# Sorted tokens of an expert layer in three groups instead of two, gated products moved from VectorE to ScalarE and GpSimd, and a new order of the work beside attention

## The chip, the cores and the metric

One core of a Trainium2 chip runs the whole program. The metric is the device time in microseconds (us) of one execution, as the median of several. The engines are named as the profile names them: PE (TensorE; PEld are its weight loads), DVE (VectorE), ACT (ScalarE), POOL (GpSimd) and SP (SyncE, which issues most DMAs).

## The reference

Input x is [1, 2048, 128], float32. Two layers, each with modulation by a vector c (shift, scale and gate rows from silu(c) @ wmod):

```python
h = layernorm(x) * (1 + ca) + sa
x = x + ga * attention0(h)       # 16 heads of 8, all 2048 keys, softmax
h = layernorm(x) * (1 + cb) + sb
x = x + gb * ffn0(h)
# second layer, its own modulation
x = x + ga * attention1(h)       # 8 query heads of 16, one key/value head, causal
x = x + gb * ffn1(h)             # x mixed with its predecessor, sigmoid(r) * (relu(k)**2 @ W_v)

def ffn0(hidden, ...):
    logits = hidden @ router_w.T                 # 16 experts, top 1
    scores = sigmoid(top logit), 0 elsewhere
    gate, up = split(einsum('nth,nhf->ntf', hidden * scores, gate_up_proj))
    routed = einsum('ntf,nfh->nth', up * silu(gate), down_proj)    # F = 128
    shared = (silu(hidden @ sg.T) * (hidden @ su.T)) @ sd.T        # SF = 512
    return shared + routed.sum over experts
```

## The kernel before, in words

The 2048 tokens are four chunks of 512. Layer 0's attention is 16 units (a chunk by four quads of heads) of 16 steps, numbered j 0 to 255; layer 1's is 8 units (a chunk by two quads) of 4 to 16 steps, 80 in all, since it is causal. One step covers 128 keys for 512 queries and 4 heads: the PE makes four transposed score tiles into PSUM banks (L1001, L1011), ACT takes their exponentials into PT (L1593), and the PE multiplies PT of the step before with the values (L1035, "pv"). So each step has four exponentials of 512 columns. Ahead of a unit, its scores are also made untransposed, for the maximum of every row: the PE fills a pair of banks (L958, L966), and DVE reduces 1024 columns (L1338). That is a "score tile"; a unit of layer 0 has 32. When the last is done, POOL splits the maxima in parts (L1872 to L1876), the PE turns them, ACT copies them (L1578) and SP writes them beside the queries. In diagonal steps of layer 1 POOL masks PT (L1772) ahead of pv.

PSUM is two pairs of banks S0, S1 for score tiles, a ring of three banks T0 to T2 for transposed scores, and O. Small jobs take either a T bank (`beside`) or a pair S (`between`).

The order is planned once by `make_plan` and every engine runs through the same list, so all queues are in order, those of POOL and SP too. A step issues its scores, up to `MOST` score tiles as `rate` asks (it looks 24 steps ahead; a unit's tiles are due `LEAD` = 3 to 5 steps before its first step), and calls `do_later`, which runs the first due entry of a book keyed by step numbers: twice a step in layer 0, three times from unit 15 of layer 0 on. `urgent` (turned maxima) comes first, the book `later` next, and `after` (the mixes of layer 1's feed-forward) last. `at_side` entries (statistics, places, scatters, fetches, gathers, accept) run without a slot. `after_chunk` books what follows when a chunk's attention is done.

For chunks 0, 1 and 2 `route` makes the second norm, the turned h, the logits and the one-hot of the best expert. After chunk 2 `sort(.., 0)` ranks the tokens of chunks 0 to 2 (group 0, 28 expert tiles of 128 rows, each tile one expert's), places and scatters them to DRAM (POOL, indirect DMA), and SP fetches each tile's expert weights (w_gate, w_up, w_down, 384 columns) into 16 slots in Wg. `experts` goes through pairs of tiles: m0 turns two tiles (PE, ACT copies 256 columns, L1676), m1 makes gate and up products into the two banks of a pair S (L1150), with ACT's tanh of the gate (L1682) and DVE's (tanh + 1) * gate and times up (L1456, L1461), and m2 is the down product (L1158), copied by ACT (L1686). SP stores, POOL gathers the rows back (L1930), and DVE accepts them into x. `shared` is the shared expert of one chunk: four `up` stages of 512 columns (PE L1106, L1107; ACT L1670; DVE L1397, L1402) and one `down` (L1116, L1407). `setup1` prepares a chunk for layer 1: accept, norm, turn, q and k projections with a split in two float16 parts, values; `ready[c]` is the step from which layer 1 may score that chunk. Group 1 is chunk 3, 20 tiles with 8 slots in the finished layer-0 keys, run in layer 1's units 3 and 4; unit 6 and 7 of layer 1 belong to chunk 3.

The core of the scheme is this:

```python
GROUPS = ((0, 12, 0, 28), (12, 16, 28, 20))     # first and last token tile, first expert tile, count
...
for p in range(n + 2):
    if g:
        at(s + int(pace * p), lambda p=p: (m0(p), m1(p - 1)), lambda p=p: m2(p - 2))
    else:
        at(s + int(pace * p), lambda p=p: (m0(p), m2(p - 2)), lambda p=p: m1(p - 1))
```

## Time and profile before

| | us |
|---|---|
| median of 3 runs | 1078.5 (1070.91 to 1096.03) |
| the profiled execution's own time | 1067.41 |
| its span in the profile | 1065.5 |
| PE, DVE, ACT, POOL busy | 922.1, 887.4, 819.6, 185.4 |

Layer 0's steps begin at 71.4 us, layer 1's at 777.3 us. The span is from the first instruction to the last; 1.9 us lie around it. A matmul's end is modelled, so a busy PE is not a PE at its peak, and a float32 product shows as two matmul rows. The mean granted clock of the TensorE was 0.963 of full speed.

### The profile page before, as it was taken

To read this page: it belongs to the slowest core of one execution; us is meant where nothing else is said; L and a number is where in the kernel's file an instruction comes from. 1 tells how busy PE (TensorE), PEld (TensorE's weight loads), DVE (VectorE), ACT (ScalarE), POOL (GpSimd) and SP (SyncE) were. 2 spreads that over 40 slices of the span, in tenths; PEclk is the share of its full clock that TensorE was granted. 3 is DMA by queue.
4 is the path that set the end of the run, shared out by engine and by line. 5 is a ranking of instruction groups with operands and counts; after the bars stand their busy time and mean duration, and the time that the engine had idled before them with its cause. 6 is when DMAs were issued, how large, how long until landed. Compare 5 with 4: busy or idle time off the path is not lost.

```text
span 1065.5 us, 22648 instructions
## 1 busy us (share of the span) xinstructions
PE 922.1 (87%) x8934; PEld 339.6 (32%) x8934; DVE 887.4 (83%) x1133; ACT 819.6 (77%) x1587; POOL 185.4 (17%) x347
## 2 busy tenths in 40 slices
PE   5998888888888888888888899899988998788888
PEld 2552222222222222222232355333333453222224
DVE  7999999999999999999998688753688767797704
ACT  4139999998999998999986588574865566566786
POOL 4233300003000003000023200331032213201112
PEclk9779999999999999999999999996989999899999
DMA  3510400000000000000000451111100341100000
GB/s 108 160 52 3 134 17 16 2 2 2 1 2 2 2 2 2 2 1 2 2 2 24 133 151 53 40 46 36 37 2 4 118 126 29 41 10 1 1 11 12
DMA packets 41385, 37.03 MB, mean 35 GB/s; under 512 B 5084, under 2 KB 39452, under 8 KB 41280
## 3 DMA queue, kind: packets, MB, share of 16 engines
q1 hardware_dynamic: 39024, 30.20, 9.8%
q0 software_dynamic: 1824, 5.25, 1.7%
q8 instruction: 72, 1.18, 0.5%
q14 instruction: 33, 0.27, 0.1%
q10 hardware_dynamic: 432, 0.13, 0.0%
HBM read 21.92 MB, written 13.30 MB: 33 GB/s over the span
## 4 chain that ended last, share of the span: by engine, by line
PE 40%; DVE 35%; ACT 17%; issue 6%; POOL 1%; DMA 1%; another core or an unknown queue 0%; ACTq 0%; DVEq 0%; SPq 0%; POOLq 0%
DVE mx L1338 30%; ACT PT L1593 12%; PE O L1035 11%; PE T L1001 7%; PE T L1011 2%; PE S L1150 2%; PE S L966 2%; PE S L1116 2%; ACT PT L1587 1%; PE S L1106 1%; PE S L958 1%; PE T L916 1%; PE O L885 1%; PE S L971 1%; PE S L1107 1%
## 5 line engine op out<-in xcount | busy, mean ns | idle before, releaser
L1338 DVE TENSOR_REDUCE mx<-S 128x2 f32<-128x1024 f32 (+2 forms) x672 | 755.6, 1181 | 64.1 <-PE S L971 23.1
L1593 ACT ACTIVATE PT<-T 128x512 f32<-128x512 f32 (+2 forms) x1280 | 674.2, 580 | 111.0 <-PE T L1011 48.3
L1035 PE MATMUL O<-PT,Va 128*9 128x256 f32 (+1 forms) x4032 | 328.1, 390 | 5.4 <-ACT Os L1627 5.4
L1001 PE MATMUL T<-Qs,Ks 26*128 26x512 f16 x1024 | 201.5, 386 | 66.2 <-ACT PT L1593 49.8
L958 PE MATMUL S<-Ks,Qs 24*128 24x512 f16 x1024 | 201.0, 392 | 7.3 <-DVE mx L1338 3.0
L1001 PEld LDWEIGHTS T<-Qs,Ks 26*128 26x128 f16 x1024 | 55.5, 91 | 290.5 <-ACT PT L1593 191.6
L1035 PEld LDWEIGHTS O<-PT,Va 128*9 128x9 f32 x4032 | 67.6, 88 | 120.0 <-issue 109.2
L1035 PE MATMUL O<-PT,V 128*17 128x512 f32 (+3 forms) x616 | 76.2, 562 | 0.4 <-POOL PT L1772 0.3
L1011 PE MATMUL T<-Qs,K 50*128 50x512 f16 (+3 forms) x256 | 47.0, 360 | 25.3 <-ACT PT L1593 24.4
L966 PE MATMUL S<-K,Qs 48*128 48x512 f16 (+3 forms) x320 | 59.3, 363 | 7.4 <-DVE mx L1338 6.1
L1872 POOL TENSOR_SCALAR n<-nm 128x16 f16<-128x16 f32 x24 | 6.7, 280 | 309.4 <-DVE nm L1346 309.4
L958 PEld LDWEIGHTS S<-Ks,Qs 24*128 24x128 f16 x1024 | 48.1, 91 | 21.4 <-DVE mx L1338 10.7
L1772 POOL TENSOR_SCALAR_AFFINE_SELECT PT<-PT 128x256 f32<-128x256 f32 x64 | 26.4, 418 | 128.8 <-ACT PT L1593 102.1
L1885 POOL TENSOR_TENSOR vw<-om,rl 128x128 f32<-128x128 f32 x16 | 6.5, 407 | 179.2 <-DVE rl L1352 179.2
L1011 PEld LDWEIGHTS T<-Qs,K 50*128 50x128 f16 x256 | 14.0, 93 | 65.1 <-issue 49.8
L1587 ACT ACTIVATE PT<-S 128x1024 f32<-128x1024 f32 (+3 forms) x32 | 27.7, 945 | 0.9 <-PE S L1011 0.9
L966 PEld LDWEIGHTS S<-K,Qs 48*128 48x128 f16 x320 | 16.1, 95 | 34.2 <-DVE mx L1338 22.9
L1106 PE MATMUL S<-hT,sgT 128*128 128x512 f32 x32 | 19.0, 676 | 4.9 <-DVE mx L1338 2.6
L1397 DVE SCALAR_TENSOR_TENSOR Vf<-Vf,S 128x512 f32<-128x512 f32 x16 | 10.9, 684 | 13.5 <-ACT Vf L1670 11.6
L1930 POOL DMA_INDIRECT XP<-sorted_y,posu x16 | 15.6, 978 | 36.6 <-DMA sorted_y<-Vf 32.5
L1670 ACT ACTIVATE Vf<-S 128x512 f32<-128x512 f32 x16 | 9.5, 594 | 16.0 <-PE S L1106 15.5
L1578 ACT ACTIVATE nrow<-T 8x512 f16<-8x512 f16 x24 | 14.1, 586 | 9.6 <-PE T L981 9.2
(325 smaller groups left out, 837.9 us busy)
## 6 DMA issues: line engine op xcount, KB each, us to landing
Wg<-in_L_ffn_experts SPq DMA_DIRECT2D x28, 192.0 KB, 2.5
Ks<-in_L_ffn_experts SPq DMA_DIRECT2D x20, 192.0 KB, 2.7
Vf<-sorted_x SPq DMA_DIRECT2D x12, 256.0 KB, 4.4
sorted_y<-Vf SPq DMA_DIRECT2D x12, 256.0 KB, 2.3
rows_q<-q SPq DMA_DIRECT2D x7, 256.0 KB, 2.3
sorted_x<-XP POOLq DMA_DIRECT2D x1, 1792.0 KB, 10.7
Qs<-nrow SPq DMA_DIRECT2D x96, 2.0 KB
Qs<-rows_q SPq DMA_DIRECT2D x8, 192.0 KB, 3.6
```

What stands on the lines that cost most here:

```text
L958: m = e.matmul(two[:, i, :], Qs[r0:r0 + 24, quad, q0:q0 + 128], Ks[r0:r0 + 24, quad, CH * kb:CH * kb + CH], start=True, stop=True, tile_po ...
L966: m = e.matmul(two[:, i, 0:n], Q1[r0:r0 + 48, 2 * quad + pair, q0:q0 + 128], K1[r0:r0 + 48, CH * kb:CH * kb + n], start=True, stop=True, t ...
L1001: m = e.matmul(bank, Ks[r0:r0 + 26, quad, keys], Qs[r0:r0 + 26, quad, CH * c:CH * c + CH], start=True, stop=True, tile_position=(r0, 0))
L1011: m = e.matmul(bank[:, lo:CH], K1[r0:r0 + 50, keys], Q1[r0:r0 + 50, 2 * quad + pair, CH * c + lo:CH * c + CH], start=True, stop=True, tile ...
L1035: m = e.matmul(acc[32 * g:32 * g + d1, lo:hi], v, PT[(2 * j + g // 2) % 4][:, p0 + lo:p0 + hi], start=fresh, stop=True, skip_group_check=n ...
L1106: e.matmul(two[:, 0, :], sgT[:, 128 * bl:128 * bl + 128], hc(c), start=True, stop=True).then_inc(gate_made, 1)
L1116: m = e.matmul(bank[:, 128 * j:128 * j + 128], ams[bl][:, 128 * j:128 * j + 128], sdT[:, bl, :], start=first, stop=True, skip_group_check= ...
L1150: m = e.matmul(two[:, h, 128 * k:128 * k + 128], w_of(g, 2 * p + k)[:, 128 * h:128 * h + 128], hS[p % 2][:, 128 * k:128 * k + 128], start= ...
L1338: e.tensor_reduce(mx[:, u % 2, h0:h0 + 2, kb], two[:, :, 0:n], AX.X, ALU.max).then_inc(free, 1)
L1587: e.activation(both, Sb[turn["st", L, j, 2 * pair][0]][:, :, lo:CH], ACT.Exp).then_inc(free, 1)
L1593: e.activation(PT[(2 * j + pair) % 4][:, CH * i + lo:CH * i + CH], bank[:, lo:CH], ACT.Exp).then_inc(free, 1)
L1772: e.affine_select(out=both, in_=both, compare_op=ALU.is_ge, fill=0.0, base=0, pattern=[[0, 2], [1, 128]], channel_multiplier=-1).then_inc( ...
```

## The change

Three groups: chunks 0 and 1 (24 expert tiles), chunk 2 (20), chunk 3 (20), 64 tiles in place of 48. Groups 0 and 1 share the 16 weight slots, group 2 has 8 as before. Shared chunks 0 and 1 are booked ten steps after the chunk's attention product y, group 0's experts 21 steps after chunk 1's; group 1 follows chunk 2, group 2 follows chunk 3. Gather and setup of a chunk are booked from its group's last m2.

m1 and `up` become two jobs of 256 columns, each in one T bank: `gate` (product, then ACT's tanh and ACT's copy into SBUF) and `lift` (product, ACT's copy), and POOL computes (tanh * gate + gate) * lift with three products or sums of 256 columns. A lift is run by the next call of `do_later` after its gate, behind `urgent` and ahead of the books. `down` becomes four jobs of 128 columns, which wait for POOL. DVE keeps only the addition of each down to x. The core of the diff:

```diff
-GROUPS = ((0, 12, 0, 28), (12, 16, 28, 20))
-NT = 48
-SLOTS = (16, 8)
+GROUPS = ((0, 8, 0, 24), (8, 12, 24, 20), (12, 16, 44, 20))
+NT = 64
+GROUP_OF = (0, 0, 1, 2)
+SLOTS = (16, 16, 8)
...
+    def gated(*a):
+        def gate():
+            P.gate[a] = len(P.gate) + 1
+            beside("gate", *a)
+            lifts.append(a)
+        return [gate]
...
+    def experts(s, g, per):
+        pieces = []
+        for p in range(n + 2):
+            if p < n:
+                pieces.append(lambda p=p: beside("m0", g, p))
+            if 0 <= p - 1 < n:
+                pieces += gated("m1", g, p - 1)
+            if 0 <= p - 2 < n:
+                pieces.append(lambda p=p: m2(p - 2))
+        def gather(s):
+            for i, c in enumerate(c for c in range(4) if GROUP_OF[c] == g):
+                at_side(s + 2 * i, lambda c=c: P.stage("gather", c))
+                setup1(s + 3 + 2 * i, c)
+        pieces[-1] = lambda: (m2(n - 1), gather(now[0] + 1))
+        for i, piece in enumerate(pieces):
+            at(s + int(i / per), piece)
     def shared(s, c, apart):
-        for bl in range(4):
-            at(s + apart * bl, lambda bl=bl: between("up", c, bl))
-        at(s + 4 * apart, lambda: between("down", c))
+        pieces = []
+        for half in range(2):
+            for bl in range(4):
+                pieces += gated("up", c, bl, half)
+            pieces += [lambda j=j: beside("down", c, j) for j in (2 * half, 2 * half + 1)]
+        for i, piece in enumerate(pieces):
+            at(s + int(i * apart), piece)
...
         elif c < 2:
             route(t + 5, c)
+            shared(t + 10, c, 3)
+            if c == 1:
+                sort(t + 11, 0)
+                experts(t + 21, 0, 1)
         elif c == 2:
             route(t + 2, 2)
-            s = sort(t + 8, 0)
-            shared(t + 7, 0, 3)
-            s = experts(s, 0, 1)
...
-            shared(s - 1, 1, 1)
-            setup1(s + 3, 0)
-            setup1(s + 5, 1)
-            shared(s + 4, 2, 1)
-            setup1(s + 9, 2)
+            sort(t + 8, 1)
+            shared(t + 9, 2, 0.7)
+            experts(t + 16, 1, 1.2)
         else:
             route(t + 1, 3, 2)
-            shared(t + 5, 3, 1)
-            s = sort(t + 5, 1)
-            s = experts(s, 1, 0.6)
-            at_side(s, lambda: P.stage("gather", 3))
-            setup1(s + 3, 3)
+            s = sort(t + 5, 2)
+            shared(t + 6, 3, 0.6)
+            experts(s, 2, 2.3)
...
+        if lifts:
+            beside("lift", *lifts.pop())
+            return
...
+                    pe.wait_ge(gated, P.gate["up", c, 3, j // 2])
                     for bl in range(4):
+                        m = e.matmul(bank[:, 0:128], ams[bl][:, 128 * j:128 * j + 128], sdT[:, bl, :], start=bl == 0, stop=bl == 3)
...
+                elif name == "gate":
+                    bank, free = filled((name,) + tuple(a))
+                    if P.gate[tuple(a)] > 2:
+                        ac.wait_ge(gated, P.gate[tuple(a)] - 2)
+                    tanh, gate, _ = gate_buffers(a)
+                    e.activation(tanh, bank[:, 0:256], ACT.Tanh, scale=0.5)
+                    e.activation(gate, bank[:, 0:256], ACT.Copy).then_inc(free, 1)
+                elif name == "lift":
+                    e.activation(lift, bank[:, 0:256], ACT.Copy).then_inc(free, 1)
...
+                    po.tick(e.tensor_tensor(tanh, tanh, gate, ALU.mult))
+                    po.settle()
+                    po.tick(e.tensor_tensor(tanh, tanh, gate, ALU.add))
+                    po.settle()
+                    e.tensor_tensor(to, tanh, lift, ALU.mult).then_inc(gated, 1)
```

## Rows read from the trace of the kernel before

**Rows 1.** Page: span and part 1 (engine, busy us, share, instructions)
```profile
span 1065.5 us, 22648 instructions
PE 922.1 (87%) x8934; PEld 339.6 (32%) x8934; DVE 887.4 (83%) x1133; ACT 819.6 (77%) x1587; POOL 185.4 (17%) x347
```

**Rows 2.** Busy time by stage: start:end length, then each engine's busy us, PEclk, DMA share, GB/s
```profile
71.40:557.80 486.40, 419.53 (x5036) 122.06 (x5038) 476.43 (x471) 458.96 (x867) 61.16 (x131) 1.00 0.05 13
263.70:300.90 37.20, 32.46 (x399) 9.02 (x398) 37.17 (x35) 35.72 (x67) 1.14 (x4) 1.00 0.01 2
557.80:673.60 115.80, 104.20 (x1008) 48.00 (x1012) 94.03 (x121) 84.50 (x174) 17.80 (x24) 0.96 0.29 85
673.60:748.80 75.20, 68.05 (x386) 26.50 (x389) 37.85 (x80) 42.77 (x79) 21.57 (x25) 0.86 0.15 40
804.10:880.80 76.70, 70.11 (x523) 35.30 (x521) 60.23 (x104) 46.81 (x110) 15.61 (x31) 0.98 0.30 87
921.40:1009.40 88.00, 70.88 (x522) 21.09 (x522) 75.98 (x88) 58.46 (x119) 10.39 (x21) 0.96 0.02 4
969.90:1065.50 95.60, 77.81 (x623) 28.38 (x621) 44.19 (x88) 71.92 (x130) 13.85 (x31) 0.98 0.02 7
```

**Rows 3.** Timeline, layer 0's full stretch: start, us, instruction; y, maxima, exponentials (ACT), tiles (DVE)
```profile
235.06 0.60 ACT L1647 ACTIVATE vw<-T 128x512 f32<-128x512 f32 x1 [0.58 <-PE T L1063]
235.55 10.63 ACT L1593 ACTIVATE PT<-T 128x512 f32<-128x512 f32 x19
...
293.76 0.59 ACT L1578 ACTIVATE nrow<-T 8x512 f16<-8x512 f16 x1 [0.18 <-PE T L981]
...
235.45 11.62 DVE L1338 TENSOR_REDUCE mx<-S 128x2 f32<-128x1024 f32 x10 [0.75 <-PE S L958]
```

**Rows 4.** Timeline of ACT where expert pairs begin, two m0 alone, then whole pairs
```profile
610.67 2.16 ACT L1593 ACTIVATE PT<-T 128x512 f32<-128x512 f32 x4 [3.56 <-PE T L1001]
612.72 0.39 ACT L1676 ACTIVATE Vf<-T 128x256 f32<-128x256 f32 x1
613.39 2.23 ACT L1593 ACTIVATE PT<-T 128x512 f32<-128x512 f32 x4 [0.28 <-PE T L1001]
616.17 1.08 ACT L1593 ACTIVATE PT<-T 128x512 f32<-128x512 f32 x2 [0.28 <-PE T L1001]
...
618.15 1.09 ACT L1593 ACTIVATE PT<-T 128x512 f32<-128x512 f32 x2 [0.38 <-PE T L1001]
...
622.05 1.09 ACT L1593 ACTIVATE PT<-T 128x512 f32<-128x512 f32 x2 [0.38 <-PE T L1001]
```

**Rows 5.** Groups by line in three stages: from 557.8, from 673.6, from 921.4 us
```profile
L1593 ACT ACTIVATE PT<-T 128x512 f32<-128x512 f32 x120 | 65.0, 594 | 20.6 <-PE T L1001 14.8 <-remote 3.2 <-issue 0.4
...
L1593 ACT ACTIVATE PT<-T 128x512 f32<-128x512 f32 x52 | 28.0, 591 | 14.1 <-PE T L1001 13.3 <-issue 0.6
L1930 POOL DMA_INDIRECT XP<-sorted_y,posu x12 | 11.6, 970 | 26.2 <-DMA sorted_y<-Vf 23.0 <-issue 3.2
...
L1338 DVE TENSOR_REDUCE mx<-S 128x2 f32<-128x1024 f32 (+3 forms) x64 | 68.8, 1120 | 10.8 <-PE S L966 6.7 <-PE S L971 3.6
```

**Rows 6.** Groups by line over the whole span: one DVE and one ACT operation of m1
```profile
L1456 DVE SCALAR_TENSOR_TENSOR Vf<-Vf,S 128x256 f32<-128x256 f32 x24 | 10.1, 421 | 10.3 <-ACT Vf L1682 10.2
L1682 ACT ACTIVATE Vf<-S 128x256 f32<-128x256 f32 x24 | 9.3, 386 | 2.5 <-PE S L1150 0.5
```

**Rows 7.** Timeline of the PE: one block's gate product, one chunk's down
```profile
559.43 1.12 PE L1106 MATMUL S<-hT,sgT 128*128 128x512 f32 x2
...
606.48 3.84 PE L1116 MATMUL S<-sdT,Vf 128*128 128x128 f32 x32
```

**Rows 8.** Timeline, POOL's products early in layer 0, and DVE's tiles beside them
```profile
82.49 0.45 POOL L1850 TENSOR_TENSOR wvv<-wvv,gH 128x128 f32<-128x128 f32 x1
84.14 4.96 POOL L1857 TENSOR_TENSOR xs<-xs,boB 128x512 f32<-128x512 f32 x4
...
80.28 10.31 DVE L1338 TENSOR_REDUCE mx<-S 128x2 f32<-128x1024 f32 x9 [0.49 <-PE S L958]
```

More of the change, by code:

```diff
@@ L204, in sort @@
         for k in range(SLOTS[g]):
-            at_side(s + 4.5 + k * (0.5 if g else 0.75), lambda k=k: P.stage("fetch", g, k, P.pvs))
+            at_side(s + 4.5 + k * (0.5 if g == 2 else 0.75), lambda k=k: P.stage("fetch", g, k, P.pvs))
         s += 4 + (t1 - t0) // 2
@@ L208, in sort @@
         return s + 2
-    def experts(s, g, pace):
-        n = GROUPS[g][3] // 2
-        def m0(p):
-            if p < n:
-                beside("m0", g, p)
-        def m1(p):
-            if 0 <= p < n:
-                between("m1", g, p)
-        def m2(p):
-            if 0 <= p < n:
-                beside("m2", g, p)
-                for k in (2 * p + SLOTS[g], 2 * p + 1 + SLOTS[g]):
-                    if k < GROUPS[g][3]:
-                        P.stage("fetch", g, k, P.pvs)
-        for p in range(n + 2):
-            if g:
-                at(s + int(pace * p), lambda p=p: (m0(p), m1(p - 1)), lambda p=p: m2(p - 2))
-            else:
-                at(s + int(pace * p), lambda p=p: (m0(p), m2(p - 2)), lambda p=p: m1(p - 1))
-        return s + int(pace * (n + 1)) + 1
@@ L350, in make_plan @@
     out = dict.fromkeys(units, 0)
-    urgent = []
+    urgent, lifts = [], []
     si = [0]
@@ L571, in make_plan @@
         J += 1
-    while later or after or light or urgent:
+    while later or after or light or urgent or lifts:
         now[0] += 1
@@ L813, in w_of, with w_there, gate_buffers @@
         def w_of(g, k):
-            return Wt[g][k % SLOTS[g]]
+            return (Wk if g == 2 else Wt)[slot_use(g, k) % SLOTS[g]]
+        def w_there(g, k):
+            n = slot_use(g, k)
+            return w_fetched[g // 2][n % SLOTS[g]], 16 * (n // SLOTS[g] + 1)
         def two_before(g, p):
-            return (g, p - 2) if p >= 2 else (0, GROUPS[0][3] // 2 - 2 + p) if g else None
+            return (g, p - 2) if p >= 2 else (g - 1, GROUPS[g - 1][3] // 2 - 2 + p) if g else None
+        def gate_buffers(a):
+            return [gates[:, P.gate[tuple(a)] % 2, i, :] for i in range(3)]
         def two_tiles(v):
@@ L1155, in pe_program @@
                     bank, full = opened(("m2", g, p))
[L1156 removed]
+                    pe.wait_ge(gated, P.gate["m1", g, p])
                     for k in range(2):
@@ L1917, in po_program @@
                     e.tensor_tensor(hv, hv, sv.unsqueeze(2).to_broadcast([128, 4, 128]), ALU.mult).then_inc(prepared, 1)
+                elif name == "lift":
+                    tanh, gate, lift = gate_buffers(a)
+                    done((name,) + tuple(a))
+                    if a[0] == "up":
+                        _, c, bl, half = a
+                        to = ams[bl][:, 256 * half:256 * half + 256]
+                        if c:
+                            passed(("down", c - 1, 2 * half + 1))
+                    else:
+                        _, g, p = a
+                        to = acS[p % 2]
+                        if two_before(g, p):
+                            passed(("m2",) + two_before(g, p))
+                    po.tick(e.tensor_tensor(tanh, tanh, gate, ALU.mult))
[3 more added lines that the diff above has]
+                    e.tensor_tensor(to, tanh, lift, ALU.mult).then_inc(gated, 1)
                 elif name == "scatter":
```

153 lines of the change are left out of this document (56 added, 97 removed).

## The prediction

> **What bounds the kernel now.** I read the page's busy shares first: DVE, ACT and PE are all above 75% of the span, POOL has 17% [rows 1]. An average over stages says little here, so the second view is the busy time by stage [rows 2]. Its bounds are starts of steps, found by counting exponentials (four per step while three T banks are in use; 120 of them in the 30 steps from 557.8 us, 52 in the 13 steps from 673.6 us [rows 5]).
> One layer-0 unit of 16 steps, with no expert work beside it, takes 37.2 us with DVE at 37.17 and ACT at 35.72 us busy: 2.32 us a step. Between the small jobs the exponentials run without a gap, 19 in 10.63 us, so four take 2.23 us; two score tiles cost DVE 2 x 1.16 us (10 in 11.62 us) [rows 3]. So ACT and DVE are both full from 71.4 to 557.8 us, and the PE has only a little room. A job beside the steps there costs what it adds to ACT, and some more, because its T bank delays the next pair of scores.
> From 557.8 to 673.6 us (shared chunk 0, 14 pairs of expert tiles) ACT is idle 31 of 115.8 us and the PE busy 104; from 673.6 to 748.8 us (shared chunks 1 and 2, setup of three layer-1 chunks) DVE is busy 37.9 of 75.2 us, ACT 42.8, the PE 68, at a mean clock of 0.86 (it falls to its lower level, 1.2 GHz) [rows 2]. This is the valley that the change can fill. At the end layer 1 is held by DVE once chunk 3 is ready: 64 score tiles in the 26 steps from 921.4 to 1009.4 us, 75.98 of 88.0 us busy [rows 2, 5].
>
> **What the steps cost now.** A small job in the full stretch: the layer's output product y leaves a gap of 0.58 us and adds its own 0.60 (start to start 0.49), some 1.1 us in all; a turned row of maxima adds 0.18 + 0.49 = 0.6 to 0.7 [rows 3]. One m0 (0.39 us on ACT) in a step moves the four exponentials from 2.23 to 2.72 and 2.78 us apart (610.67, 613.39, 616.17), that is +0.5, with a gap of 0.28 us behind the copy, since the next scores wait for their bank [rows 4]. A step that carries a whole pair (m0, m1, m2) takes 3.90 us (618.15 to 622.05) [rows 4]: +1.67.
> Before, by subtraction: 115.8 - 30 x 2.32 - 14 x 1.67 = 22.8 us for shared chunk 0 with ranks and places, of which I give 17 to the chunk. 75.2 - 13 x 2.32 = 45 us for shared chunks 1 and 2 (27 together) and the setups (18). In layer 1, 76.7 - 17 x 2.2 = 39 us for shared chunk 3 (17), ten pairs (19) and three small jobs (3). These splits are my choice; the sums are the rows'.
>
> **Part by part.** (a) *More pairs.* 48 expert tiles become 64: 32 pairs, of which 22 fall in layer 0 (14 before) and 10 in layer 1 (10 before).
> (b) *A pair's jobs.* m0 and m2 stay; m1 becomes a gate (two ACT ops on 256 columns) and a lift (one). ACT ops of that size take 0.386 us (tanh) and 0.39 (copy) [rows 4, 6], 0.35 from start to start by the overlap of 0.04 that the exponentials show. Five of them: 1.75 us, the low end, with no gap at all. By the m0 rows a job of one op costs 0.5; the gate has 0.7 us of ACT, and its second op fills the gap. I take 0.5 + 0.7 + 0.5 + 0.5 = 2.2 us, the rows being nearest to the jobs themselves. High end 2.6 (all jobs at the 0.6 to 0.7 of the turned row). What goes is 0.84 us of DVE (two operations like L1456's 0.42 [rows 6]), worth nothing where ACT is the later of the two. Layer 0: 22 x 2.2 - 14 x 1.67 = +25. Layer 1: 22 - 19 = +3.
> (c) *A shared chunk.* Eight gates and lifts and four downs: PE for a half, two products of 256 columns, about half of 1.12 us each; a down has 4 of the 16 products that took 3.84 us [rows 7], so 0.96, and costs what y does. 8 x 1.2 + 4 x 1.1 = 14.0 us. Three chunks in layer 0: 42 against 44, -2. Chunk 3: 14 against 17, -3. Ends: ACT alone, 8 x 1.05 + 4 x 0.5 = 10.4; high 17.
> (d) *GpSimd's products.* They lie beside everything unless somebody waits. POOL takes 0.45 us for 128 columns and 1.24 for 512 [rows 8]; between them 0.7 for 256, three in a row with two settles 2.2 us a piece. ACT's next gate but one and m2 wait for it three or more jobs later, hidden (a job is 1.3 us or more, slots included). The first down of a half comes right behind its last lift. With pieces three steps apart (chunks 0, 1) that is hidden; at 0.7 and 0.6 steps (chunks 2, 3) PE waits 2.2 + 1.5 us less one slot, some 2.3 us, and behind it wait the next scores, so ACT too: 2 x 2.3 = +4.6 us in each layer. Behind a waiting lift on POOL stand masks, the parts of the maxima, scatters and gathers; low end nothing, high end +10 (eight masked steps with shared chunk 3 or experts beside them, 1.2 us each).
> (e) *Setups.* Those of chunks 0 to 2 stay in layer 0, at full clock rather than 0.86: -2.
> (f) *The order, layer 0.* Shared chunks 0 and 1 and 12 pairs move into the full stretch before 557.8 us. They find no idle ACT there, so they cost the prices above, and the valley's steps get shorter by as much as left them. That is in (a) to (c): by them layer 0 is 25 - 2 + 4.6 - 2 = 25.6 us longer.
> (g) *The order, layer 1.* Group 2 has 30 pieces at 2.3 a step plus 10 lifts, and shared chunk 3 has 12 pieces and 8 lifts. `do_later` runs one job a call, three calls a step here, and lifts go ahead of the book. From step 9 of layer 1: 20 + 40 jobs + some 9 others = 69, / 3 = 23 steps, so the last m2 stands near step 32 (24 or 25 before, where one call issued m0 and m1 together). The gather comes a step later, accept three behind it, rows three more, and `ready` four after: step 43 or 44 against 33 or 34. Units 6 and 7 of layer 1 (64 tiles) can't be scored until then. These ten steps cost ACT about 2.3 us each, 23 to 25 us, with DVE idle. From there 32 tiles at 68.8 / 64 = 1.08 us [rows 5] and 5 us for the maxima's way, about 40, then units 6 and 7 as now from 969.9 us on, 95.6: 136 against the 144.1 us that lie behind 921.4 us now. Net 24.5 - 8 = +17 us. The mixes only change places. Low end 5 (the book catches up and DVE's work was late anyway), high end 27.
> The 16 added fetches of weights and the rows of group 1 travel while the stages that fetch now show a DMA share of 0.3 at most [rows 2]: hidden.
>
> The sum: 25.6 (layer 0) + 3 - 3 + 4.6 + 17 (layer 1) = +47 us on the profiled execution's 1067.4 us (its span of 1065.5 and 1.9 around it), 1114 us. That execution is 1% below the median of the runs, 1078.5, and 0.3% below the fastest of them, 1070.9. I keep 1114 and leave that 1% to the range.
> Ends: all low ends, 22 x 1.75 - 23.5 = +15, shared -13, (e) -2, layer 1 -1.5 - 6.6 + 0 + 5: about -3 us, 1064. All high ends: 22 x 2.6 - 23.5 = +34, shared 51 - 44 = +7, 4.6, layer 1 +7 + 0 + 4.6 + 10 + 27: +94, 1161.
>
> *A rule weighed.* While POOL added without a pause, 84.14 to 89.1 us, DVE's score tiles ran 9 in 10.31 us, 1.15 each, as with POOL idle (1.16) [rows 3, 8]. The Trainium skill (GPSIMD Engine Reference, section 8, Key points) says that GpSimd shares its SBUF interfaces with VectorE and contends with VectorE instructions that run in a two-port mode or have two SBUF inputs. By that rule the 192 added GpSimd products would lengthen DVE's few additions from SBUF, not the tiles, which read PSUM; the trace agrees for the tiles and no row shows the additions. By the rule the sum would grow by a microsecond or two, by the row by nothing.
>
> **The rivals.** (1) *The valley is filled: faster.* ACT's work by pace in layer 0 would be 16 x 37.2 + 15.6 (the routes' and y's extra up to 557.8, 486.4 - 203 x 2.32) + 22 x 1.75 + 24 x 1.05 + 3 x 3 = 683 us, ending at 754 instead of 777.3 if ACT never waits, -23; and chunk 3's lateness hidden by tiles of unit 4 and 5 spread over those steps. 1067.4 - 23 + 2 = 1046 us. For it: ACT idles 31 and 32 us in the two valley stages [rows 2]. Against: every small job in the full stretch leaves a gap [rows 3, 4]. It decides from the point where nothing but ACT's own time counts: no gap behind any job, the downs and the products of the setups hidden as well (at the low ends above they are not, and 1064 is no gain to tell). Chance 0.17.
> (2) *Even.* Gaps half as large as the rows show and a chunk 3 ready five steps late: pairs at 1.9 (+18), shared -6, waits +5, layer 1 -3 + 8: +16 or less, 1075 to 1085. It also stands for a change that does not deliver what it moves: layer 1's scores are held back to three to five steps ahead of use, so earlier chunks bring no earlier scores. Chance 0.23.
> (3) *POOL holds the others.* In layer 1 a gate is issued every 2.8 us against POOL's 2.2, and masks and gathers stand in the same queue: a gather that waits for the stored rows (26.2 us of POOL's idle time in the valley [rows 5]) holds masks and so PV. High ends of (d) and (g): +80, 1147. Chance 0.15.
>
> **How the numbers follow.** Forecast 0.45, the three above 0.17, 0.23, 0.15. What can be told from no change here is 2%, so the bounds are 1057 and 1100 us. Slower: forecast and (3), 0.60; within 2%: 0.23; faster: 0.17. The forecast's own range is 1100 to 1130. The range goes down to 1060, which takes in (2) and the low end, and up to 1150 for (3).
>
> **What would show it.** Right: exponentials of steps with one job 2.7 to 3.0 us apart between 260 and 560 us; ACT busy up by about 60 us, DVE down by about 40; DVE idle in the layer-0 stretch; first L1 exponentials near 800 us; PE waiting for POOL before the downs of chunks 2 and 3; a stretch in layer 1 with no score tiles, then tiles back to back. Wrong: layer 0 ending before 780 us (the gaps are hidden), or score tiles of unit 6 beginning by step 36 of layer 1.

## The result, and the profile after

The changed kernel's median is 1153.2 us of four runs (1141.62 to 1169.57), beside 1074.7 for the kernel before on the same chip: a ratio of 1.066, with a 95% interval from 1.048 to 1.084. (Some executions run at a lower granted clock and longer; ratios and their intervals compare the others alone, here 1141.62 and 1142.14 us with 1063.19, 1070.91 and 1078.5, while a time given in us is the median of all.) It is slower, by more than the forecast's 47 us. The profiled executions stand 1141.62 against 1067.41 us, +74.2; spans and steps below are of these. The kernel before had medians of 1060.8, 1072.3 and 1067.7 in the three sets of runs below, so versions are compared by their ratios to it, and stages by the profiled executions.

The page's busy shares after (as [rows 1]), and of its groups the score tiles and the first of POOL's three products (busy us, mean ns, idle time before them and what ended it):

```profile
span 1139.9 us, 23579 instructions
PE 968.0 (85%) x9166; PEld 361.6 (32%) x9166; DVE 872.0 (76%) x1079; ACT 867.1 (76%) x1756; POOL 326.1 (29%) x540
...
L1354 DVE TENSOR_REDUCE mx<-S 128x2 f32<-128x1024 f32 (+2 forms) x672 | 767.3, 1182 | 157.2 <-PE S L981 69.5
...
L1920 POOL TENSOR_TENSOR Vf<-Vf 128x256 f32<-128x256 f32 x64 | 46.7, 730 | 225.9 <-ACT Vf L1665 225.9
```

ACT has 47.5 us more work and POOL 140.7, DVE only 15.4 less; the span grew by 74.4. So more ACT work explains at most two thirds. DVE's score tiles (L1354) are the same 672, and DVE now stands idle 157.2 us before them, while POOL mostly waits for the next lift (225.9).

Busy time by stage, after (columns as in [rows 2]). The bounds are the same steps as in the first fence of numbers below: steps 142 to 202 of layer 0, 203 to 231, 232 to 245; then layer 1's steps 8 to 32, 33 to 41, 42 to 47, 48 to the end:

```profile
421.50:628.50 207.00, 180.41 (x1800) 70.51 (x1803) 165.61 (x195) 171.58 (x355) 75.45 (x105) 0.95 0.19 54
628.50:736.40 107.90, 91.80 (x892) 39.23 (x894) 78.39 (x87) 84.79 (x187) 42.88 (x61) 0.95 0.21 60
736.40:784.90 48.50, 43.73 (x426) 17.37 (x418) 28.33 (x45) 39.12 (x79) 16.18 (x26) 1.00 0.09 27
839.00:954.50 115.50, 100.33 (x678) 44.41 (x674) 63.46 (x90) 76.23 (x185) 56.81 (x86) 0.93 0.21 61
954.50:991.00 36.50, 26.02 (x174) 10.51 (x174) 12.18 (x38) 24.83 (x51) 13.68 (x21) 1.00 0.15 40
991.00:1044.30 53.30, 37.30 (x182) 7.95 (x180) 44.30 (x44) 11.03 (x25) 5.29 (x12) 0.55 0.02 5
1044.30:1139.90 95.60, 78.68 (x620) 28.36 (x617) 41.94 (x86) 72.02 (x130) 13.94 (x31) 0.96 0.02 7
```

In the first of them neither ACT (172 of 207 us) nor DVE (166) is full any more, where both were before. In the fifth DVE works 12.2 of 36.5 us, in the sixth 44.3 of 53.3 while ACT works 11.0: two stages that should lie beside each other come one behind the other.

The length of each stage, in us, from the start of one step's first exponential to that of another (layer 0's steps have their number, layer 1's an L1 before it):

```
                    0-77 78-111 112-141 142-202 203-231 232-245 246-255 L1.0-7 8-32  33-41 42-47 48-end  span
before             187.2   79.4   73.8   146.0   112.1    78.9    28.5   26.7 114.7  33.0  18.2  95.6  1065.5
after              187.3   91.7   73.9   207.0   107.9    48.5    27.2   26.9 115.5  36.5  53.3  95.6  1139.9
e5_changed         187.3   91.6   73.9   200.1   107.7    47.0    26.0   28.9 113.0  39.4  52.7  95.9  1132.2
e1_l1_fused        188.2   91.7   73.8   201.9   107.8    46.9    26.0   29.0 118.7  39.5  25.6  97.8  1118.3
e2_order_only      186.5   90.5   73.8   199.7    97.3    51.6    26.0   26.7 108.2  36.0  42.4  96.3  1106.4
e3_pool_one        187.3   91.7   73.8   202.6    98.6    46.9    26.0   26.8 108.0  36.4  53.4  95.5  1117.1
e4_no_gate_copy    187.1   90.5   73.9   197.5   105.2    46.6    26.0   29.0 112.3  37.1  53.4  95.6  1122.8
e6_downs_later     187.1   91.6   73.9   201.7    98.7    46.9    26.0   25.7 114.5  43.4  52.7  95.9  1129.5
e7_downs_accept_l1 187.4   91.6   73.9   199.7   100.6    42.1    31.3   29.0 113.7  44.1  32.0  98.3  1112.3
e8_shared_early    187.2   90.3   73.8   156.9    95.3    70.7    28.5   26.6 116.3  34.8  18.2  95.6  1064.2
e9_tiles_48        186.5   91.6   73.9   200.9   107.1    52.0    42.1   25.7 112.4  41.3  42.2  96.3  1143.4
e10_late_before    187.1   79.5   73.8   146.0   111.8    80.6    28.5   28.3 108.1  35.7  46.8  97.5  1093.7
e11_all_mended     187.1   91.6   73.9   202.5    98.6    47.0    27.3   29.0 113.0  42.5  23.3  96.1  1103.3
e12_order_mended   186.5   90.6   73.8   200.8    99.3    49.9    26.0   27.5 108.7  33.9  19.2  99.6  1087.2
```

The start before step 0 (71.4 us before, 68.6 after) is the rest of each span. The loss has two places. Layer 0 is 37.6 us longer: +12.3 where shared chunk 0 now stands (steps 78 to 111), +61.0 in steps 142 to 202, and only -34.6 in the two stages of the valley. Layer 1 is 39.6 us longer, and 38.6 of that lie in steps 33 to 47.

The rows e5_changed and e1_l1_fused have the changed kernel's plan in layer 0, so they say how far one profile of it differs from another: layer 0 takes 743.5, 733.6 and 736.3 us, that is 37.6, 27.7 and 30.4 more than before. Most of the first profile's surplus is in steps 148 to 152, 19.9 us where e5 takes 14.4 for the same work (columns as above, first profile, then e5):

```profile
439.20:459.10 19.90, 16.79 (x133) 4.29 (x136) 14.20 (x15) 12.77 (x26) 9.99 (x13) 0.74 0.47 133
```

```profile
439.20:453.60 14.40, 12.85 (x133) 3.94 (x136) 13.60 (x15) 12.63 (x26) 10.20 (x13) 1.00 0.38 114
```

The granted clock stood at 0.50, the lower level of 1.2 GHz, from 447.2 to 457.4 us there, and again from 590.6 to 600.8; in the kernel before it is 1.00 through all of steps 142 to 202.

### The profile page after: what moved, and what is told of

It reads as the page before. It is cut to its first block, busy times and chain, and to the rows that moved or that the text cites. A ratio compares the mean times of both kernels' runs of the same rounds, so it can differ in the third digit from the quotient of the medians.

```text
span 1139.9 us, 23579 instructions
## 1 busy us (share of the span) xinstructions
PE 968.0 (85%) x9166; PEld 361.6 (32%) x9166; DVE 872.0 (76%) x1079; ACT 867.1 (76%) x1756; POOL 326.1 (29%) x540
## 4 chain that ended last, share of the span: by engine, by line
PE 43%; ACT 24%; DVE 20%; issue 7%; POOL 4%; DMA 1%; SPq 0%; another core or an unknown queue 0%; ACTq 0%; POOLq 0%; DVEq 0%
ACT PT L1584 17%; DVE mx L1354 17%; PE O L1058 13%; PE T L1024 9%; PE T L1034 2%; PE T L1167 2%; PE S L989 2%; PE T L1129 2%; PE T L1136 2%; PE T L1175 2%; ACT PT L1578 1%; ACT Vf L1661 1%; PE S L994 1%; PE S L981 1%; PE O L908 1%
## 5 line engine op out<-in xcount | busy, mean ns | idle before, releaser
L1354 DVE TENSOR_REDUCE mx<-S 128x2 f32<-128x1024 f32 (+2 forms) x672 | 767.3, 1182 | 157.2 <-PE S L981 69.5
L1058 PE MATMUL O<-PT,Va 128*9 128x256 f32 x4088 | 329.0, 389 | 7.1 <-ACT Os L1618 3.9
L1024 PEld LDWEIGHTS T<-Qs,Ks 26*128 26x128 f16 x1024 | 58.0, 91 | 269.1 <-ACT PT L1584 145.2
L1920 POOL TENSOR_TENSOR Vf<-Vf 128x256 f32<-128x256 f32 x64 | 46.7, 730 | 225.9 <-ACT Vf L1665 225.9
L1058 PE MATMUL O<-PT,V 128*17 128x512 f32 (+3 forms) x616 | 81.4, 594 | 1.3 <-POOL PT L1761 1.2
L989 PE MATMUL S<-K,Qs 48*128 48x512 f16 (+3 forms) x320 | 66.3, 410 | 13.8 <-DVE mx L1354 13.1
L1924 POOL TENSOR_TENSOR Vf<-Vf 128x256 f32<-128x256 f32 x64 | 46.7, 729 | 5.0
L1922 POOL TENSOR_TENSOR Vf<-Vf 128x256 f32<-128x256 f32 x64 | 46.4, 725 | 5.0
L1569 ACT ACTIVATE nrow<-T 8x512 f16<-8x512 f16 x24 | 14.0, 583 | 28.2 <-PE T L1004 27.7
L1660 ACT ACTIVATE Vf<-T 128x256 f32<-128x256 f32 x64 | 24.7, 386 | 13.4 <-PE T L1129 7.1
L1665 ACT ACTIVATE Vf<-T 128x256 f32<-128x256 f32 x64 | 25.0, 391 | 12.5 <-PE T L1129 7.6
L1167 PE MATMUL T<-Vf,Wg 128*128 128x128 f32 x176 | 31.3, 301 | 0.0
```

The source lines that it names most:

```text
L989: m = e.matmul(two[:, i, 0:n], Q1[r0:r0 + 48, 2 * quad + pair, q0:q0 + 128], K1[r0:r0 + 48, CH * kb:CH * kb + n], start=True, stop=True, t ...
L1024: m = e.matmul(bank, Ks[r0:r0 + 26, quad, keys], Qs[r0:r0 + 26, quad, CH * c:CH * c + CH], start=True, stop=True, tile_position=(r0, 0))
L1058: m = e.matmul(acc[32 * g:32 * g + d1, lo:hi], v, PT[(2 * j + g // 2) % 4][:, p0 + lo:p0 + hi], start=fresh, stop=True, skip_group_check=n ...
L1167: m = e.matmul(bank[:, 128 * k:128 * k + 128], w_of(g, i)[:, w0:w0 + 128], hS[p % 2][:, 128 * k:128 * k + 128], start=True, stop=True)
L1354: e.tensor_reduce(mx[:, u % 2, h0:h0 + 2, kb], two[:, :, 0:n], AX.X, ALU.max).then_inc(free, 1)
L1920: po.tick(e.tensor_tensor(tanh, tanh, gate, ALU.mult))
```

## The experiments

**Set 1: lateness, order, products, copy.** Beside the kernel before at 1060.8 us.

e1: in layer 1 the lift is issued in the same call as its gate, and group 2's book is drawn at 4 pieces a step, so that its last m2 comes four steps earlier (step 27 instead of 31).

```diff
             beside("gate", *a)
-            lifts.append(a)
+            if now[0] >= STEPS0:
+                beside("lift", *a)
+            else:
+                lifts.append(a)
...
-            experts(s, 2, 2.3)
+            experts(s, 2, 4)
```

> The changed kernel, but in layer 1 a gate's lift is issued in the same call as the gate, and group 2's pieces are booked at 4 a step instead of 2.3: its last m2 moves from step 31 to step 27 of layer 1, chunk 3's projections from 37 to 34. Lateness theory (the steps without score tiles in layer 1 cost their own length): layer 1 shorter by 3 or 4 steps of 4 us each, 12 to 15 us, with layer 0 unchanged at 743 us. Rival (layer 1 is longer because the jobs cost more there, not because of the order): within 4 us of the changed kernel.

1117.3 us, ratio 1.055 (1.048 to 1.061). Layer 1 is 17.2 us shorter than in the changed kernel: steps 42 to 47 take 25.6 us for 53.3, and the other stages 10.5 more between them; layer 0 stays long. The same work, issued earlier, gives back nearly half of layer 1's loss.

e2: three groups, 64 tiles and the new order, with the gating of the kernel before.

```diff
-                pieces += gated("m1", g, p - 1)
+                pieces.append(lambda p=p: between("m1", g, p - 1))
...
+        pieces = [lambda bl=bl: between("up", c, bl) for bl in range(4)] + [lambda: between("down", c)]
         for i, piece in enumerate(pieces):
-            at(s + int(i * apart), piece)
+            at(s + int(i * apart * 2.4), piece)
```

> The kernel before with the three groups, the 64 tiles and the booked places of the changed kernel, but with the gate made as before (pair of S banks, ACT's tanh, two DVE operations, m1 and up in one call of 512 or 2 x 256 columns). Theory that number and place of the pairs carry the loss in layer 0: 22 pairs at about 1.8 us and the waits of the setups stay, so about 1110 to 1125 us. Rival, that the new way of making the gate carries it: 1070 to 1090 us. If DVE's work in the full stretch is the dearer: above 1140 us.

1115.4 us, 1.058 (1.048 to 1.067), span 1106.4. Of the 74 us in the spans 41 are there without any gating on ACT and POOL: +19.5 in layer 0 and +21.4 in layer 1. The gating has the other 33, or 26 against the changed kernel's second profile (e5). By the ratios its share is smaller, 0.9 to 1.4% of the time, and those intervals overlap.

e3: POOL makes one of its three products; left out is the gate's own factor, so the output is tanh times lift.

```diff
-                    po.tick(e.tensor_tensor(tanh, tanh, gate, ALU.mult))
-                    po.settle()
-                    po.tick(e.tensor_tensor(tanh, tanh, gate, ALU.add))
-                    po.settle()
```

> The changed kernel with only the last of GpSimd's three operations per piece (tanh times lift), so the gated value leaves out the gate itself. Theory: GpSimd is on the path only at the downs of chunks 2 and 3 and beside the scatters, worth 15 to 20 us of the 74. Rival (GpSimd's in-order queue holds the others throughout): 35 us or more less. Second rival (GpSimd hidden everywhere): within 4 us.

1120.4 us, 1.059 (1.052 to 1.065). The span is 15 to 23 us below the changed kernel's two profiles: chiefly 9 in steps 203 to 231 and 5 to 7.5 in L1.8 to 32, the stages of shared chunks 2 and 3. The steps of chunk 0, where pieces stand three apart, did not move (91.7 both times). So GpSimd's products cost nothing where pieces are far apart, and something where somebody waits for the last of them.

e4: ACT leaves out the gate's copy, and POOL takes the lift in its place (the gate's factor is left out of the output in this way).

```diff
-                    e.activation(tanh, bank[:, 0:256], ACT.Tanh, scale=0.5)
-                    e.activation(gate, bank[:, 0:256], ACT.Copy).then_inc(free, 1)
+                    e.activation(tanh, bank[:, 0:256], ACT.Tanh, scale=0.5).then_inc(free, 1)
```

> The changed kernel without ACT's copy of the gate (64 operations of 0.39 us); GpSimd's first two operations take the lift in its place, so the values are others. If a job's price is ACT's own time: 64 x 0.35 = 22 us less, and steps with one gate fall from 2.81 to 2.45 us. If the price is the T bank's way round (PE, ACT, PE), the second op fills a gap: the step with one gate stays above 2.75 us and the time within 6 us of the changed kernel.

1128.2 us, 1.068 (1.060 to 1.077). Taking 64 copies of 0.39 us (25 us) off ACT left the ratio where the whole change has it. The span is 9 to 17 us lower, less than the copies last. A step with one gate takes 2.79 us without the copy and 2.91 with it, so the expectation's second branch held: the copy mostly fills a gap that is there anyway. It is not what the change suffers from.

**Set 2: the downs, the gather, and the valley.** Beside the kernel before at 1072.3 us. e5 is the changed kernel once more, as the measure for e6 and e7.

> The changed kernel once more, beside the next three on one chip: 1140 to 1155 us, 6 to 8% over the kernel before.

1140.4 us, 1.072 (1.059 to 1.086), its span 1132.2. Of the 7.7 us below the first profile 6.9 lie in steps 142 to 202 (200.1 for 207.0 us), in the steps shown above: this much one profile can differ from another in that stage.

e6: with pieces close together, the first two downs are booked three pieces later, and the last two three places later.

```diff
-            pieces += [lambda j=j: beside("down", c, j) for j in (2 * half, 2 * half + 1)]
+        downs = [lambda j=j: beside("down", c, j) for j in range(4)]
+        gap = 0 if apart > 1 else 3
+        pieces = pieces[:4 + gap] + downs[:2] + pieces[4 + gap:] + [None] * gap + downs[2:]
...
+            if piece:
```

> The changed kernel with the downs of shared chunks 2 and 3 put three pieces behind the last lift of their half, all else as it is. Theory: PE waits there for GpSimd with the next scores behind it (9.4 us in the step with the first down of chunk 2, 7.4 in the step with the last two, 8.3 and 7.4 in layer 1): 12 to 18 us less, most of what the run with one GpSimd product gave back. Rival (GpSimd holds ACT by the wait of the gate, or masks): under 5 us.

1125.4 us, 1.059 (1.048 to 1.069). This is the wait that e6 takes away, in the changed kernel's timeline: the PE, then ACT, then POOL, about the first down of shared chunk 2.

```profile
655.21 2.05 PE L1136 MATMUL T<-sdT,Vf 128*128 128x128 f32 x8 [4.55 <-POOL Vf L1924]
...
657.83 1.08 ACT L1584 ACTIVATE PT<-T 128x512 f32<-128x512 f32 x2 [6.62 <-PE T L1024]
...
650.44 1.01 POOL L1930 DMA_INDIRECT sorted_x<-XP,posu  x1 [0.16 <-issue]
651.75 0.96 POOL L1930 DMA_INDIRECT sorted_x<-XP,posu  x1 [0.30 <-issue]
652.74 0.73 POOL L1920 TENSOR_TENSOR Vf<-Vf 128x256 f32<-128x256 f32 x1
653.55 0.72 POOL L1922 TENSOR_TENSOR Vf<-Vf 128x256 f32<-128x256 f32 x1
654.35 0.72 POOL L1924 TENSOR_TENSOR Vf<-Vf 128x256 f32<-128x256 f32 x1
```

ACT had the last lift ready by 649.9 us, but two scatters of group 1 stand before it in POOL's queue, so the product ends at 655.1. The PE stands 4.55 us at the down, the next scores stand behind it, and ACT stands 6.62 us. Over the whole trace the PE waits four times for POOL at a down (us in total, times, longest); in e6 it waits there once, 0.7 us:

```profile
PE T L1136 <- POOL Vf L1924: 10.5, 4, 4.5
```

With the wait gone, steps 203 to 231 are 9.0 us shorter. Little of it reaches the end of the span (1129.5 for 1132.2). Of what is given back, 4.0 us lie in steps 33 to 41 of layer 1, where both kernels have the same plan; e5 first, e6 second:

```profile
944.20:983.60 39.40, 29.21 (x174) 10.78 (x174) 12.14 (x38) 24.93 (x50) 13.68 (x21) 0.91 0.14 37
```

```profile
937.50:980.90 43.40, 34.43 (x174) 13.21 (x174) 12.15 (x38) 24.93 (x50) 13.79 (x21) 0.72 0.12 33
```

The work is the same and the granted clock isn't: 43.4 us at 0.72, 39.4 at 0.91, and 36.5 at 1.00 in the first profile of the changed kernel. e6's profiled execution was also the longest of its four, e5's the shortest. The medians differ by 15 us, with ratio intervals that overlap. So the wait is real, and its value at the end is between 3 and 15 us.

e7: e6, with the setups of groups 0 and 1 booked three steps later behind their gather, and with e1's edit.

```diff
-                setup1(s + 3 + 2 * i, c)
+                setup1(s + (3 if g == 2 else 6) + 2 * i, c)
```

> The changed kernel with the downs later, the accept of chunks 0 to 2 three steps further behind their gathers, and layer 1's fused calls of e1. Theory: the parts add up, 12 to 18 for the downs, 5 to 8 for the accepts (DVE stood before a gather that had not landed), 17 in layer 1: 1105 to 1115 us, still above the kernel before by 3 to 4%, since 8 more pairs at 2.2 us and a late chunk 3 are left. Rival (they all treat one stall, which moves on): no better than e1, within 5 us of it.

1113.2 us, 1.047 (1.038 to 1.055). Its gain over e6 lies again in L1.42 to 47 (32.0 for 52.7). The later setups bring almost nothing in steps 142 to 202 (199.7 for 201.7), where 5 to 8 us were expected: in e6 steps 194 to 196 take 6.6, 4.6 and 7.6 us, here 2.3, 2.7 and 3.3, but the stall moves with the setups to steps 198 and 199 (5.6 and 8.4 us, 5.8 and 3.0 in e6). Group 1's setup only moves from one stage to the next (42.1 and 31.3 for 46.9 and 26.0).

e8: the kernel *before*, with shared chunks 0 and 1 moved out of the valley into the full stretch, a block every six steps, and nothing else.

```diff
         elif c < 2:
             route(t + 5, c)
+            shared(t + 10, c, 6)
...
-            shared(t + 7, 0, 3)
...
-            shared(s - 1, 1, 1)
```

> The kernel before, with two groups, 48 tiles and its own gate, and only shared chunks 0 and 1 booked ten steps after their chunk's y, one block every 14 steps, out of the valley into the full stretch. Theory: a shared chunk costs some 12 us there and 14 to 17 in the valley at a lower clock, so 5 to 10 us less than the kernel before. Rival (DVE is full there, so a block adds its two DVE operations and the wait in the pair of S banks, 4 us or more each): 5 to 10 us more.

1065.9 us, 1.002 (0.994 to 1.011): no difference, so neither the gain nor the loss that was expected. Its two stages in the full stretch, and the two of the valley:

```profile
257.20:347.50 90.30, 82.44 (x883) 26.03 (x878) 84.67 (x87) 78.35 (x147) 3.63 (x11) 1.00 0.01 2
421.30:578.20 156.90, 140.12 (x1568) 44.03 (x1570) 148.82 (x152) 140.53 (x265) 10.87 (x23) 1.00 0.01 2
578.20:673.50 95.30, 86.71 (x924) 39.11 (x921) 84.50 (x108) 79.37 (x164) 17.78 (x24) 0.96 0.36 104
673.50:744.20 70.70, 60.78 (x382) 21.14 (x378) 34.77 (x75) 43.55 (x82) 20.82 (x25) 0.83 0.16 43
```

Each chunk costs 10.9 us where it now is, and the valley is 16.8 and 8.2 us shorter where they were: +21.8 against -25.0. The valley's idle ACT is not room that earlier work frees; a step there is as long as its jobs make it, and gets shorter as they leave.

**Set 3: lateness alone, 48 tiles, and all together.** Beside the kernel before at 1067.7 us.

e9: the changed kernel with 16 expert tiles a group, 48 as before.

```diff
-STORED = (16 * 6, 16 * 5, 16 * 5)
+STORED = (16 * 4, 16 * 4, 16 * 4)
...
-GROUPS = ((0, 8, 0, 24), (8, 12, 24, 20), (12, 16, 44, 20))
-NT = 64
+GROUPS = ((0, 8, 0, 16), (8, 12, 16, 16), (12, 16, 32, 16))
+NT = 48
```

> The changed kernel with 16 expert tiles in each of its three groups, 48 in all (these inputs need just 16 in each; a guarantee for all inputs takes the 24 and 20). Six pairs fewer in layer 0, two in layer 1. Price theory (a pair costs 2.2 us in layer 0 wherever it stands): layer 0 13 us shorter, and layer 1 by 5 us plus two steps of lateness at 4 us, together 20 to 26 us less than the changed kernel. Rival (pairs are cheap beside attention, the waits are what costs): under 10 us less.

1131.5 us, 1.061 (1.055 to 1.068): a gain of about 1% on e5's 1.072, half of what eight fewer pairs at 2.2 us plus an earlier chunk 3 should give, and with intervals that overlap. This miss has two parts. Steps 142 to 202 hold four pairs fewer and are no shorter (200.9 for 200.1). The stall at group 0's accept now stands in steps 180 to 187, and with the steps between they take 38.0 us, the granted clock at 0.50 from 554.0 to 567.7; steps 148 and 149 take 8.8 us for 6.6. And in the profiled execution, 13.6 us above the runs' median, steps 246 to 255 took 42.1 us instead of 27.2, with the same instructions. The stage in e9 and in the changed kernel:

```profile
783.40:825.50 42.10, 42.10 (x270) 8.82 (x268) 19.90 (x21) 22.77 (x43) 0.74 (x3) 0.52 0.01 1
```

```profile
784.90:812.10 27.20, 27.01 (x270) 8.10 (x268) 19.62 (x21) 22.68 (x42) 0.85 (x4) 0.94 0.09 20
```

The granted clock was 0.52 for ten steps, near the lower level of 1.2 GHz, and the PE was busy for every microsecond of them.

e10: the kernel *before*, with its second group of experts drawn half as fast in layer 1. Nothing is added.

```diff
-            s = experts(s, 1, 0.6)
+            s = experts(s, 1, 1.2)
```

> The kernel before with group 1's experts booked at 1.2 steps a pair instead of 0.6, nothing else: last m2 at step 30 of layer 1 instead of 25, chunk 3's projections at 36 instead of 29. Lateness theory: six or seven steps later, each losing 3 to 4 us once units 6 and 7 wait: 18 to 25 us more than the kernel before, with layer 0 as it is. Rival (tiles catch up at five a step, ACT's steps are only moved): within 6 us.

1091.5 us, 1.025 (1.019 to 1.031), and 28.2 us in the span, 2.7 in steps 33 to 41 and 28.6 in 42 to 47. The timeline of DVE shows the pattern of the changed kernel: a stretch without tiles before 945 us, then tiles back to back.

```profile
910.73 2.35 DVE L1338 TENSOR_REDUCE mx<-S 128x2 f32<-128x1024 f32 x2
...
936.29 0.26 DVE L1357 RECIPROCAL rl<-S 128x16 f32<-128x16 f32 x1 [1.36 <-PE S L1044]
...
945.00 7.42 DVE L1338 TENSOR_REDUCE mx<-S 128x2 f32<-128x1024 f32 x7 [5.78 <-PE S L966]
...
953.67 10.00 DVE L1338 TENSOR_REDUCE mx<-S 128x2 f32<-128x256 f32 x10 [1.25 <-PE S L971]
```

A late chunk 3 costs this by itself, with the old groups, the old gating and the old shared chunks.

e11: e6, e9 and e1 together, setups three steps later. 

> The changed kernel with 48 tiles as in e9, downs and accepts later and layer 1's fused calls as in e7. If the causes add: e7's 1.0465 less 20 us, so 1.5 to 3.5% over the kernel before. What is left would be the gate's own price in ACT and T banks (2.2 against 1.67 us a pair) and one step or two of lateness. If something else is at work: 4% or more.

1104.8 us, 1.040 (1.032 to 1.047). If the causes added, 1.5 to 3.5% over the kernel before were expected; they don't. Layer 0 takes 728.1 us with 16 pairs, where e7 takes 726.6 with 22.

e12: e2 with e9's 48 tiles and group 2 drawn at 4 a step: the new order with its lateness mended, and no gating on ACT and POOL. 

> e2 (three groups and the new order, the gate as before) with 48 tiles and group 2 booked at 4 pieces a step. If number of pairs and lateness are the order's whole loss: within 1.5% of the kernel before, and 10 us or more below e11. If moving work into the full stretch itself loses or gains: outside of that, above or below.

1096.0 us, 1.029 (1.015 to 1.044). Layer 1 takes 288.9 us, where the kernel before takes 288.2: the order's whole loss there was lateness. Layer 0 still takes 726.9 for 705.9 us. The expectation, within 1.5% if pairs and lateness were the order's whole loss, failed: something in layer 0 is left over. No version tried beats the kernel before.

## Why the prediction was right or wrong

The direction, the engines and both mechanisms were right; the size was not: +47 forecast, +74 in the profiled executions (+67 in the second profile of the changed kernel). The two executions of 1142 us lie inside the range, the median of all four, 1153, just above its 1150. The range reached that far for the sake of rival (3), GpSimd, and not of what happened; that part of the hit is luck. The term that was mis-sized is (g), +17 for a measured +38.6. The steps:

**(b) A pair's jobs: right.** 2.2 us was the price. Between 552 and 568 us of the changed kernel:

```profile
552.82 2.24 ACT L1584 ACTIVATE PT<-T 128x512 f32<-128x512 f32 x4 [0.28 <-PE T L1024]
555.18 0.38 ACT L1660 ACTIVATE Vf<-T 128x256 f32<-128x256 f32 x1
555.46 0.38 ACT L1661 ACTIVATE Vf<-T 128x256 f32<-128x256 f32 x1
555.73 1.09 ACT L1584 ACTIVATE PT<-T 128x512 f32<-128x512 f32 x2
556.82 0.38 ACT L1665 ACTIVATE Vf<-T 128x256 f32<-128x256 f32 x1
557.38 1.09 ACT L1584 ACTIVATE PT<-T 128x512 f32<-128x512 f32 x2 [0.17 <-PE T L1024]
558.59 0.38 ACT L1675 ACTIVATE Vf<-T 128x256 f32<-128x256 f32 x1
559.01 2.24 ACT L1584 ACTIVATE PT<-T 128x512 f32<-128x512 f32 x4
561.14 0.39 ACT L1671 ACTIVATE Vf<-T 128x256 f32<-128x256 f32 x1
561.80 2.24 ACT L1584 ACTIVATE PT<-T 128x512 f32<-128x512 f32 x4 [0.28 <-PE T L1024]
```

A step with one gate takes 2.91 us (552.82 to 555.73), one with lift and m2 3.28 (555.73 to 559.01), one with m0 2.79 (559.01 to 561.80), over 2.23 without a job: 0.68 + 1.05 + 0.56, 2.3 a pair when spread so; with two jobs a step 2.2. The gap of 0.28 us behind a lone m0 is there, 0.17 behind a lift; the gate's two operations leave none, as argued. With one of them gone a part of the gap comes back, which fits e4's small gain.

**(a) More pairs: right in size.** I took each layer-0 step's excess over 2.23 us and shared it out evenly among the jobs that the plan puts in that step. How the part beside the pairs splits further depends on how jobs are counted, so it is one column:

```
              pairs   us of pairs   all else   layer 0's excess
before          14        23.0        112.0        135.0
after           22        48.7        123.9        172.6
e5_changed      22        48.6        114.1        162.7
e2_order_only   22        42.2        112.3        154.5
e9_tiles_48     16        35.5        147.7        183.2
e12_order_mended 16       31.0        125.0        156.0
```

Pairs: +25.7 us against the +25 forecast. This is an accounting: where pairs were taken out by experiment (e9, e11), layer 0 did not get shorter.

**(c), (d), (e) together: too low in layer 0.** Forecast -2 + 4.6 - 2 = +0.6; all but the pairs grew by 11.9 us in the first profile and by 2.1 in the second, and the 9.8 between them are those of one execution against another, the lower clock in steps 148 to 152 above all. Within the small sum two terms were off. One fault was in the subtraction on the side of before. From two sums in the valley I gave the shared chunks 17 + 27 and said that the split was my choice; e8 took two of them out and found 16.8 and 8.2. Chunk 0 was right and chunk 1 was overrated by 5; if chunk 2, which no run moved, is like it, the three were some 33 us where I had 44. The price after, 12.3 us for chunk 0, was nearer the forecast's 14. So a term of -2 was, by this estimate, some +4. The wait at the downs was predicted as 2 x 2.3 us in each layer, 9.2 in all; the PE waited 10.5. But the two scatters in front made one of the waits 4.55, and the 6.6 us of ACT behind it were dearer than the PE's own wait: 9.0 us of the stage by e6. Where group 0 is accepted, in steps 192 and 193 of the first profile (194 to 196 in e5), the engines stood for more than the gather. The timelines of DVE, the PE and ACT there:

```profile
588.38 0.76 DVE L1459 TENSOR_TENSOR XP<-XP,gB 128x512 f32<-128x512 f32 x1 [0.75 <-DMA XP<-sorted_y,posu]
...
589.86 0.62 PE L1058 MATMUL O<-PT,Va 128*9 128x256 f32 x8 [3.08 <-issue]
...
593.56 1.08 ACT L1584 ACTIVATE PT<-T 128x512 f32<-128x512 f32 x2 [2.31 <-remote]
```

DVE waits 0.75 us for the gather, but the PE stood 3.08 us and ACT 2.31 for nothing that the profile names. The forecast gave this accept no wait. Setups booked later (e7) carried the stall with them and did not remove it; what it is, no run shows.

**(f) The valley isn't filled: right, and shown** for the two shared chunks by e8, which also disposes of rival (1).

**(g) Chunk 3 is late: the mechanism right, the size half.** Last m2 in step 31 (32 forecast), rows in step 37, first tile of unit 6 in step 42 (43 or 44). Yet +38.6 us instead of +17, and every microsecond of it before step 48: from there to the end it is 95.6 us in both kernels, as the forecast used. Two terms were mis-sized. The nine steps 33 to 41 took 36.5 us, 4.06 each, not 2.3 to 2.5. They hold chunk 3's accept, turns and projections and seven mixes, which the prediction let "only change places": before, steps 33 to 41 had four mixes beside 25.4 us of DVE's work and took 33.0 us; now there are three more and DVE works 12.2 us. That the mixes are what the steps wait for is my reading; no run took them out. And unit 6's tiles and maxima took 53.3 us, not 40. The timeline of DVE, with ACT's and PE's next turn, shows how:

```profile
1019.08 10.93 DVE L1354 TENSOR_REDUCE mx<-S 128x2 f32<-128x768 f32 x10 [0.61 <-PE S L994]
1030.05 0.22 DVE L1362 TENSOR_REDUCE nm<-mx 128x16 f32<-128x64 f32 x1
1030.18 7.20 DVE L1354 TENSOR_REDUCE mx<-S 128x2 f32<-128x1024 f32 x7
1037.76 2.90 DVE L1354 TENSOR_REDUCE mx<-S 128x2 f32<-128x256 f32 x3 [0.38 <-PE S L994]
...
1038.79 0.59 PE L1004 MATMUL T<-idb,n 128*8 128x128 f16 x4
1043.71 0.61 PE L1034 MATMUL T<-Qs,K 50*128 50x512 f16 x2 [4.33 <-DMA Qs<-nrow]
...
1039.41 0.59 ACT L1569 ACTIVATE nrow<-T 8x512 f16<-8x512 f16 x1 [17.26 <-PE T L1004]
```

The maxima are complete at 1030.3 us. Their turn on the PE stands in the plan behind ten tiles of unit 7, which DVE must empty first, so it comes at 1038.8, and with the write beside the queries unit 6 begins at 1044.3: 14 us where I had 5. The granted clock was 0.55 in this stage, but DVE was busy 44.3 of its 53.3 us, so a slow PE can have cost at most the other 9. (With the same DVE work, 22.6 us, this stage took 25.6 us at 0.84 in e1 and 23.3 at 1.00 in e11.) In the kernel before exponentials of unit 5 still run while the maxima of unit 6 are made. e1 and e10 show the lateness by itself (-17.2 and +28.2 us), e12 that it is all of the order's loss in layer 1.

**The rivals.** (3), POOL holds the others, is partly true: two of its three products are the 15 to 23 us of e3, less than the order's 41. (2), even, fell. Of the marks set down: ACT busy +47.5 (60 forecast), DVE -15.4 (40), first exponential of layer 1 at 812 (800). DVE fell less partly because its 672 score tiles, as long as before (1182 ns for 1181) but less often back to back, where one overlaps the next, count 767.3 us where they had 755.6; the rest of the 40 was counted too high.

**Open.** In e12, layer 0 keeps +21 us with 16 pairs instead of 14. The accounting puts 8.0 on the pairs (1.94 us each when their jobs stand one in a step, 1.64 when packed three in one) and 13.0 on all else. A third group sorts and is accepted once more; and the granted clock was 0.93 in steps 142 to 202 of e12, 1.00 in those of the kernel before. Either can hold a part of it, and no run isolates one. Nor did any run say why the stall at group 0's accept costs more in e9, where it comes sooner.

## What to carry to other kernels

Before you move work into a stage that looks idle, or out of it, move it alone: e8 shows that a stage with 30 us of idle ACT was no reservoir, since in an in-order schedule a stage is as long as its jobs. When a helper splits one job into several and jobs are drawn so many a step, count the steps until the *last* one, and ask what waits for it: here the first score tile of the last chunk went from step 34 of layer 1 to step 42, and that cost more than the added pairs. Price a late start by what stands alone in the gap and again by what stands in the queues when it ends, not by the mean step. And before two profiles are subtracted, look at the granted clock of the stage and at a second profile: the same steps took 36.5 to 43.4 us here.
